# Graph attention's edge pass: the linear part of the logits moves from VectorE to GpSimd

## The reference

```
xl = x @ Wl[k] + bl[k]
xr = x @ Wr[k] + br[k]
ef = ea2 @ We[k]
m = jax.nn.leaky_relu(xl[src2] + xr[dst2] + ef, SLOPE)     # SLOPE = 0.2
logit = m @ att[k]
alpha = _segment_softmax(logit, dst2, n)
out = segment_sum(xl[src2] * alpha[:, None], dst2, n) + b_out[k]
h = out + x ... layer norm, relu
```

## Time and profile before

| | us |
|---|---|
| median of three runs | 1982.47 (1979.96 to 1986.04) |
| the profiled execution | 1988.3 |
| its span, first to last instruction | 1986.6 |
| TensorE busy in the span | 1866.3 (94%) |
| VectorE busy | 955.5 (48%) |
| GpSimd busy | 320.6 (16%) |
| mean granted TensorE clock | 0.977 of full speed |
| gathers of layer 0, first to last start | 579.95 to 671.80 |
| gathers of layer 1 | 767.14 to 861.46 |
| gathers of layer 2 | 955.21 to 1048.89 |

### The profile page before, as it was taken

How to read it: one execution, slowest core, us unless ns; L and a number is a source line. 1 busy time by engine, 2 the same in 40 slices (tenths; PEclk the granted TensorE clock), 3 DMA queues, 4 the chain that set the end, 5 groups by cost and what they waited for, 6 DMA issues and landing times. The chain is left out here.

```text
span 1986.6 us, 27055 instructions
## 1 busy us (share of the span) xinstructions
PE 1866.3 (94%) x8836; PEld 1038.3 (52%) x8836; DVE 955.5 (48%) x2860; ACT 505.0 (25%) x1388; POOL 320.6 (16%) x343
## 2 busy tenths in 40 slices
PE   7999998999899999999998799879789999999999
PEld 4464557677544434533453333335435444578876
DVE  9662643000179887997799611156532223331102
ACT  1171641111134352234224412127110000010000
POOL 0000001334327404720571000000000000010001
PEclk9999999999999999999999899989899999999999
DMA  4102019998277406730678189944352232149884
GB/s 169 59 17 75 1 47 392 398 339 318 39 260 225 131 1 199 209 89 2 181 208 292 63 302 387 386 137 152 128 191 74 90 144 108 40 153 390 327 324 153
DMA packets 180664, 357.47 MB, mean 180 GB/s; under 512 B 29072, under 2 KB 38560, under 8 KB 180524
## 3 DMA queue, kind: packets, MB, share of 16 engines
q1 hardware_dynamic: 157548, 285.42, 40.0%
q0 software_dynamic: 22976, 70.23, 12.1%
HBM read 333.91 MB, written 21.69 MB: 179 GB/s over the span
## 5 line engine op out<-in xcount | busy, mean ns | idle before, releaser
L1256 PEld LDWEIGHTS ps<-tokT,w 128*128 128x128 f32 x2304 | 259.8, 192 | 11.4 <-issue 6.7
L1256 PE MATMUL ps<-tokT,w 128*128 128x128 f32 x2304 | 260.6, 275 | 3.8 <-DVE tokT L1406 2.4
L1729 POOL DMA_INDIRECT w<-xl_d,src_i x216 | 215.0, 995 | 290.5 <-DMA xl_d<-XL 222.7
L1825 PE MATMUL ps<-XP,wide 128*128 (+1 forms) x456 | 185.2, 507 | 0.0
L1830 PE MATMUL ps<-w,ident 128*128 128x512 f32 x270 | 140.7, 602 | 8.7 <-DMA w<-xl_d,src_i 8.5
L1825 PEld LDWEIGHTS ps<-XP,wide 128*128 128x128 f32 x456 | 81.4, 188 | 72.7 <-issue 67.4
L1940 ACT ACTIVATE wide<-oht 128x128 fp32r<-128x128 bf16 x228 | 68.1, 308 | 198.4 <-PE ps L1830 178.5
L1275 PE MATMUL ps<-w,O 128*128 128x512 f32 x256 | 112.5, 597 | 0.0
L1491 POOL DMA_INDIRECT spread_d<-N,slot x12 | 11.8, 981 | 583.0 <-DVE slot L1363 580.0
L2102 DVE SCALAR_TENSOR_TENSOR w<-ps,w 128x512 f32<-128x512 f32 x144 | 98.1, 681 | 5.2 <-PE ps L1830 5.0
L1425 DVE TENSOR_TENSOR hT<-act,ps 128x512 f32<-128x512 f32 x20 | 13.7, 687 | 178.0 <-ACT act L1311 178.0
(11 more groups left out here) (534 smaller groups left out, 3029.6 us busy)
## 6 DMA issues: line engine op xcount, KB each, us to landing
w<-L_ffn_W SPq DMA_DIRECT2D x16, 2048.0 KB, 14.1
w<-L_ffn_W SPq DMA_DIRECT2D x8, 4096.0 KB, 18.0
w<-fc1T SPq DMA_DIRECT2D x32, 1024.0 KB, 14.4
w<-fc2T SPq DMA_DIRECT2D x30, 1024.0 KB, 14.3
w<-L_ffn_w_down SPq DMA_DIRECT2D x10, 2048.0 KB, 14.9
w<-L_ffn_w_gate SPq DMA_DIRECT2D x20, 1024.0 KB, 9.5
w<-L_ffn_w_up SPq DMA_DIRECT2D x20, 1024.0 KB, 12.2
w<-L_ffn_w SPq DMA_DIRECT2D x8, 2048.0 KB, 13.4
```

The costliest lines, as they stand in the source:

```text
L1256: m = pe.matmul(k.ps[:, 1 + (q * ins + i) % 4, s * P:(s + 1) * P], self.W1[u][i][:, f, (q * T + s) * P:(q * T + s + 1) * P], self.tokT[:, ...
L1729: gp.indirect_dma_start(self.G[:, u, :], None, k.xl_d, bass.IndirectOffsetOnAxis(ap=k.src_i[:, i:i + 1].bitcast(U32), axis=0)).then_inc(k. ...
L1825: m = pe.matmul(bank, self.wide[:, i % DEEP, :], self.XP[:, q].rearrange("p t n -> p (t n)")[:, bass.ds(at, D)], start=False, stop=(q == 1 ...
```

## The change

The linear part is made by GpSimd. `linear` of `edge_logits` is gone, and a function `linear_part` with the same addition is called from `pool`. It stands ahead of every fourth gather from tile 16 on and takes the four tiles that are 16 to 13 ahead of that gather. The last four calls of a layer (there are 19) stand behind the last gather. The call first waits that the rows of its four tiles have landed, and from the third one on that VectorE has made the logits of the call but one before, because `part` now has two buffers. VectorE's `logits` reads the buffer in turn. A gather that follows still waits for `linear`, which is now GpSimd's own signal, and for `product`. For a tile whose row VectorE adds it also waits for `summed`, which `linear` had covered before.

```diff
-        self.part, self.wc = sb(c, k, "part", [P, QUAD]), sb(c, k, "wc", [P, 2])
+        self.part, self.wc = sb(c, k, "part", [P, 2, QUAD]), sb(c, k, "wc", [P, 2])
...
+                if i % QUAD == 0 and i >= FAR_AHEAD:
+                    self.linear_part(gp, l, i - FAR_AHEAD + QUAD)
                 if i >= T + FAR_AHEAD:
                     gp.wait_ge(self.product.sem, self.product.at(EA * l + i - FAR_AHEAD + 1))
+                    if self.by_vector(i - FAR_AHEAD):
+                        gp.wait_ge(self.summed.sem, self.summed.at(self.sums(l, i - FAR_AHEAD)))
                     gp.wait_ge(self.linear.sem, self.linear.at(self.QUADS * l + (i - FAR_AHEAD) // QUAD + 1))
                 gp.indirect_dma_start(self.G[:, u, :], None, k.xl_d, ...).then_inc(k.pool_slot[u].sem, 16)
+
+            for i in range(EA - FAR_AHEAD + QUAD, EA + 1, QUAD):
+                self.linear_part(gp, l, i)
+
+    def linear_part(self, gp, l, i):
+        if i == QUAD:
+            gp.wait_ge(self.rows_ready.sem, self.rows_ready.at(T * (l + 1)))
+        for j in range(i - QUAD, i):
+            self.landed(gp, l, j)
+        q = self.QUADS * l + i // QUAD - 1
+        if q >= 2:
+            gp.wait_ge(self.logit.sem, self.logit.at(q - 1))
+        s = (i - QUAD - T) % FAR_AHEAD
+        own = self.XL[:, :, D] if i == QUAD else self.G[:, s:s + QUAD, D]
+        gp.tensor_tensor(self.part[:, q % 2, :], own, self.eac[:, i - QUAD:i], ALU.add).then_inc(self.linear.sem, 1)
...
-        def linear(i):
-            s = (i - QUAD - T) % FAR_AHEAD
-            own = self.XL[:, :, D] if i == QUAD else self.G[:, s:s + QUAD, D]
-            v.tensor_tensor(self.part[:], own, self.eac[:, i - QUAD:i], ALU.add).then_inc(self.linear.sem, 1)
...
-            v.tensor_tensor(self.L[:, i - QUAD:i], self.part[:], self.sdot[:, i - QUAD:i], ALU.add
+            part = self.part[:, (self.QUADS * l + i // QUAD - 1) % 2, :]
+            v.tensor_tensor(self.L[:, i - QUAD:i], part, self.sdot[:, i - QUAD:i], ALU.add
...
             quad = i % QUAD == 0 and i > 0
-            if quad:
-                linear(i)
             if i >= LAG:
                 lowest(i - LAG)
             dot(i)
             if quad:
                 logits(i)
-        linear(EA)
         lowest(EA - LAG)
```

More of the change, by code:

```diff
@@ L1963, in row_statistics @@
         k, mean, var = self.k, self.ahead.mv[:, t, 0:1], self.ahead.mv[:, t, 1:2]
-        total, square, low = self.mc[:, t:t + 1], self.mrest[:, t:t + 1], self.part[:, t:t + 1]
+        total, square, low = self.mc[:, t:t + 1], self.mrest[:, t:t + 1], self.part[:, 0, t:t + 1]
         a.wait_ge(self.x_out.sem, self.x_out.at(t + 1))
@@ L2103, in dot @@
                                    accum_out=self.sdot[:, i:i + 1]).then_inc(self.dotted.sem, 1)
-        def linear(i):
-            s = (i - QUAD - T) % FAR_AHEAD
-            own = self.XL[:, :, D] if i == QUAD else self.G[:, s:s + QUAD, D]
-            v.tensor_tensor(self.part[:], own, self.eac[:, i - QUAD:i], ALU.add
-                            ).then_inc(self.linear.sem, 1)
         def logits(i):
```

## The result

The changed kernel took 2039.94 us (median of 4 runs, 2037.62 to 2044.52), the kernel before in the same rounds 1984.26. The ratio is 1.0287, 95% interval 1.0266 to 1.0308: 55.7 us slower. The forecast was 32 us slower, at 2014.5, and its range ended at 2038. The profiled execution has a span of 2040.0 us against 1986.6, 53.4 more.

What follows compares the result with a forecast made beforehand. GpSimd's stream of gathers was taken to bound each layer. 3 x 0.36 + 42 x 0.82 - 1.24 - 1.62 - 0.68 = +32.0 us on the 1982.5 median gave 2014.5, range 1990 to 2038.

Steps and rivals of the forecast that it cites:

- The stream: GpSimd's run of gathers in each layer: additions lengthen it, removed waits shorten it; +32.0 us over three layers.
- s: Time from the end of a gather to the start of the addition behind it, taken as 0.16 us.
- d: Duration of one addition on GpSimd, taken as 0.20 us.
- r: Time from an addition's end to the start of the next gather, which waits for it, taken as 0.76 us.
- c: Cost of one addition in GpSimd's stream, s + d + r less the usual 0.30: 0.82 us, for 42 additions.
- not slower: Rival, chance 0.09: additions fit into the 0.30 us gap behind a gather, price 0; -2.8 us, 1979.7.
- The wait at tile 20: GpSimd's wait for VectorE's linear part there goes: 1.24 us in layer 1, 1.62 in layer 2, nothing in layer 0.
- the list of what costs nothing: VectorE's lost additions, its 6 us stand at layer 0's first logits, landing and buffer waits, last addition: no cost.
- The last addition: At a layer's end it waits for tile 75's landing and is ready before that tile's dot product ends.
- The short release: Rival, chance 0.17: a gather behind its own engine's signal starts after 0.28 us, c is 0.34; +11.8, 1994.
- Held up by VectorE: Rival, chance 0.11: VectorE's two-SBUF-input instructions delay every addition by 0.52 us; +23 more, 2038.
- The lower clock: Rival, chance 0.03: TensorE granted 1.2 instead of 2.4 GHz half of the time; +85, 2100.

Runs made afterwards that it cites:

- copy: Kernel before with all its VectorE work; GpSimd also makes the additions at the change's places, with the change's wait, into an unread tile; 2018.77 us, ratio 1.015.
- ten: near with each addition between the second and third gather of a group, 10 tiles on; 1988.46 us, ratio 1.0027.
- near: Changed kernel with the additions 8 tiles on in GpSimd's order instead of 16, in four buffers; 1991.34 us, ratio 1.0034.
- buffers: Changed kernel with four buffers of the linear part instead of two, additions where they were; 2039.25 us, ratio 1.0275.
- near_wait: near, with GpSimd also waiting for each addition's own signal before it goes on; 2001.53 us, ratio 1.007.
- wait_first: Changed kernel with the gather's wait for `linear` moved ahead of its waits for `product` and `summed`; 2016.02 us, ratio 1.0167.
- hold: Kernel before plus one wait: VectorE makes a group's logits only when the tile eight on has landed; GpSimd untouched; 2004.93 us, ratio 1.0092.
- mid: Changed kernel with the additions 12 tiles on in GpSimd's order, in four buffers; 1998.48 us, ratio 1.0068.

## Why the prediction was wrong

- **The bound** was right for the kernel before: the last gather's issue sets when a layer ends. Where the stream grew the time grew with it (copy), and relieving VectorE of 57 additions gave nothing (ten). In the changed kernel it no longer holds, as the third point says.
- **The stream** was right in sum, +31.6 against 32.7 forecast (32.0 with the 0.68 of layer 2 taken off), and that is partly luck. s is 0.02 instead of 0.16, d 0.21 instead of 0.20, r 0.77 instead of 0.76, so c is 0.02 + 0.21 + 0.77 - 0.30 = 0.70 and not 0.82. The first addition of a layer cost 0.02 + 0.21 + 0.15 - 0.30 = 0.08, not 0.36, and so did most additions of near and ten: just the price up to which the "not slower" rival was said to decide. Together that is 5.9 us less than forecast. The wait at tile 20 went wholly, as forecast. What filled the gap was not in the sum: the long gathers (35 instead of 18, busy time +2.7 us) and three gaps, of 0.32 us over the usual at tile 32 of layer 0, 1.66 at tile 45 of layer 1 and 0.20 at tile 71 of layer 2.

```profile
843.49 0.96 POOL L1733 DMA_INDIRECT w<-xl_d,src_i  x1 [0.78 <-PE ps L1850]
846.41 0.95 POOL L1733 DMA_INDIRECT w<-xl_d,src_i  x1 [1.96 <-issue]
```

  The two at tiles 45 and 71 stand at the same tiles in all five kernels in which a gather waits for an addition just made (the change, buffers, copy, near_wait, wait_first), and in none of the others. Their cause is open.
- **What failed** is the list of what costs nothing, in two sentences: that the removed work "only makes VectorE wait longer for tiles", and, for layer 0's first logits, that VectorE stands about 6 us and "the delay is covered by the slower stream". The first stand is there (4.89 us until 594.18). But I treated it as a single event after which VectorE catches up. The addition of every group stands 11 tiles late in GpSimd's order, so VectorE meets the same wait at 42 of the 57 groups, and never gets to the "about four tiles behind the stream" on which I also built the buffer wait. My own numbers had it: the addition that logits at iteration 64 need stands behind the last gather, and VectorE then has eleven tiles at 1.17, 12.9 us, against a lag of 5.3 to 6.0 before: 7 us a layer at least, 21 in all. It measured 22.9, and hold shows the term by itself, +20.3 in the lag and 19.9 in the time.
- **The last addition** "is ready in time": true, and beside the point. Behind the last gather VectorE has eleven tiles left, and its work, not GpSimd's, ends the layer.
- **The short release**, 0.28, was a rival at 0.17, weighed by whether the signal leaves the engine. Neither that nor the number of semaphores decides: near_wait and wait_first get 0.27 from the same signal and as many waits. The order in which the waits are written does. The number adds little: behind two waits with the late one last it is 0.75 to 0.77, behind three 0.77 to 0.79.
- **Held up by VectorE**: in the change additions take 0.21 at the median and 0.32 at most, not 0.52 more, because none begins in the first half of a VectorE instruction with both inputs in SBUF; gathers do and are held up instead. With the additions elsewhere the rival's price is there: twelve of near's took 0.28 to 0.77 (below). The lower clock did not come: 0.969 against 0.977.
- Of the signs that I had named, "VectorE and TensorE wait for landings all through the second half" was false, and this was the one that told the missing cost apart. "Catches up" was false with it. The 6.0 us for four gathers and an addition came (6.07), and the last gathers start 11.7, 10.4 and 9.5 us later after the first ones, where 10 to 12 was named.

## What to carry to other kernels

Work that is moved to an in-order engine is ready when that engine gets to it, not when its inputs are: count how many instructions stand between, and compare with how many tiles the consumer is behind, for every iteration and above all for the last. If the consumer is then held, what it still has to do after the last input is added to the end of the loop. Where several waits stand ahead of one instruction, try the one that is satisfied last as the first: in this kernel that one line was worth 24 us.

## What was not expected of the hardware

- A gather behind an addition's late signal starts 0.27 or 0.28 us after the addition when that wait is the first written (all 42 of wait_first), and 0.75 to 0.79 when it is the last of two or three (41 of the change's 42; the other took 1.08). Behind an addition whose gather waits for nothing late the gap is 0.15, and between two gathers 0.30. That a satisfied wait behind the late one costs less than one ahead of it is measured; why is not.
- A gather that starts while VectorE is in the first 0.5 us of a dot product with both inputs in SBUF (`w<-w,w`, 0.68 us) ends 1.50 us after that instruction's start, wherever in it it began: 603.47 and 603.72 + 1.25 = 604.97, 608.28 and 608.47 + 1.32 = 609.79 in the rows above, 839.64 and 839.68 + 1.47 = 841.15 in the earlier trace rows. Of the gathers of before and after that began within 0.35 us of such a start, all 53 with over 1.2 us fit this to 0.01, and one, begun 0.01 us after VectorE's, took 0.94 while VectorE's instruction took 0.73. In all ten traces 251 gathers began 0.03 to 0.50 us after such a start, and every one ended 1.49 to 1.53 us after it.
- The additions are held in the same way, where they meet such an instruction. In near, near_wait, copy, mid, buffers and ten 50 of them began between 0.04 us before and 0.48 us after its start, and every one ended 0.72 to 0.75 us after that start, wherever it began. One of near's, in the timelines of GpSimd and VectorE:

```profile
816.77 0.77 POOL L1751 TENSOR_TENSOR part<-w,eac 128x4 f32<-128x4 f32 x1
...
816.81 0.69 DVE L2122 SCALAR_TENSOR_TENSOR w<-w,w 128x512 f32<-128x512 f32 x1
```

  The Trainium skill, "SBUF — State Buffer", "Who interferes with whom", has this contention for a GpSimd instruction that reads SBUF, and the additions bear it out. The same section infers, for VectorE's `tensor_tensor`, that descriptor generation is exempt. The prediction took the long gather to contradict that. But a gather also has its index list, `src_i`, in SBUF, so the rule itself may cover it, and no run here separates reading the indices from writing descriptors.
- Additions on GpSimd start 0.02 us behind a gather: the 0.30 between gathers belongs to the gather that comes, and a short operation fits partly into it, 0.02 + 0.21 + 0.15 = 0.38 in place of 0.30.
